# Second mixture of a decoder kernel: GpSimd issues the experts' row gathers further ahead of the scatters

## The chip, the cores and the metric

The kernel runs on one core of one Trainium2 chip. The metric is device time in microseconds (us) of one execution. A core has five instruction streams that matter here: TensorE (PE) for matmuls, VectorE (DVE), ScalarE (ACT), GpSimd (POOL) and SyncE (SP). POOL and SP start DMA transfers; the core's 16 DMA engines carry them out. POOL is the only one that issues indirect transfers, which take their row numbers from a tile of indices: a gather reads 128 rows of 1 KB out of DRAM into a tile, a scatter writes the 128 rows of a tile to rows of DRAM.

## What is computed

Two decoder layers, post-norm, over `x` of shape 8 x 256 x 256. Each has an attention, a cross-attention and a mixture of experts, each followed by a residual sum and a layer norm. The change lies in the mixture of the second layer only:

```python
probs = jax.nn.softmax(x @ gate_w.T, axis=-1)          # x: 2048 tokens x 256
top2_w, top2_idx = jax.lax.top_k(probs, 2)             # each token picks 2 of 8 experts
cap = int(1.25 * N / E)                                # 320 rows for each expert
buf = zeros((E, cap + 1, H)).at[a_e, p].set(x_a)       # the rows of each expert
h = silu(einsum('ech,efh->ecf', buf, w1) + b1)
y = einsum('ecf,egf->ecg', h, w2) + b2
contrib = y[a_e, p] * (a_w * valid)[:, None]           # back to the tokens, weighted
out = contrib.reshape(N, 2, H).sum(axis=1)
```

## The kernel before

All engines run programs written out by hand, with semaphores between them. Everything up to the last cross-attention takes the first 1,050 us or so and is the same in both kernels. Then comes the second mixture.

**The tiles.** The 8 experts have 320 rows each, so 2560 rows, which lie in 20 tiles of 128 rows. Two experts share five tiles: an even expert needs tiles 0 to 2 of its five, an odd one tiles 2 to 4. `tiles_of(e, True)` says which tiles are gathered for expert `e`: three for an even expert, two for an odd one (the third is there already). `tiles_of(e, False)` says which tiles are complete and can be scattered once expert `e` is computed: two for an even one, three for an odd one.

**TensorE**, for each expert `e`: wait for the weights (`t_w`), compute the hidden units (L1973, 8 matmuls of 320 columns, raising `e_u` after the fourth and the eighth), turn the rows of expert `e+1` (`turn1`, L1957, which waits for the gathers by `t_in{e % 4}` and raises `e_X`), wait for ScalarE's activation (`e_h`), compute the output (L1983, 12 matmuls, raising `e_y`). **VectorE** copies the turned rows (L1315), spreads some weights (L1332), and adds the bias to the output (L1321), which writes the tiles `y1t` and raises `e_ys`. **ScalarE** applies the activation (L782); it waits for `e_u`, and for `e_y` of the expert two before.

**GpSimd** issues the transfers of rows (L1468 to L1485). It waits once for the indices and for the rows that SyncE sent to DRAM (`sent1`). Then it issues the gathers of experts 0 to `XBUFS - 1`, that is of four experts (10 transfers). Then, for each expert, it waits for `e_ys` and scatters the complete tiles, and after it gathers for expert `e + 4`. Its queue is strictly in order. All 20 gathered tiles have places of their own in `x1t`, as have the 20 of `y1t`; nothing is written twice, so that only the four counting semaphores `t_in0` to `t_in3` are shared by two experts each.

**SyncE** loads the weights of experts 0 to 3 ahead of all this, those of expert `e + 4` when `e_ys` says that expert `e` is done (L584 to L587, four transfers, two of 256 KB, one of 128 KB and a small one), waits until all 20 scatters have landed (`e_out`), fetches the rows back in the order of the tokens (L596), and stores the result (L600).

After the last expert TensorE adds the residual (L1990), runs some matmuls that only keep it busy (L2008), and mixes the fetched rows (L1998).

Of the kernel before, what the change touches and what calls it, by code (L numbers as in the profile page):

```python
# [32 lines left out]
E, FH = 8, 512  # L33
# [16 lines left out]
XBUFS = 4  # L50
# [3 lines left out]
HOTS = 2 * EARLY  # L54
LATE_CHOOSE, LATE_RANK, LATE_HOTS, LATE_TABLE, LATE_QUANTA, LATE_RAW, LATE_INDEX, LATE_WEIGHTS = 0, 2, 3, 5, 6, 8, 8, 9
FAR = 128 * P
HIDDEN = 3
IDLE, IDLE_SPLIT, IDLE_CLIP = 96, 4, (4, 6)
IDLE_TURN, IDLE_LAYERS, IDLE_ROWS, IDLE_SCORES, IDLE_RESULT, IDLE_MIXED, IDLE_ROUTE = 4, 50, 20, 4, 12, 24, 2
# [171 lines left out]
def build_program(nc, dram, out, early0, sent0, sent1, outs0, outs1):  # L231
    with ExitStack() as ctx:
# [5 lines left out]
        def S(name):  # L238
            if name not in sems:
                sems[name] = ctx.enter_context(nc.semaphore(name))  # L240
            return sems[name]
# [212 lines left out]
        def tiles_of(e, gathered):  # L454

            first = PAIR1 * (e // 2)
            cut = PAIR1 // 2 + (1 if gathered else 0)
            return range(first + cut, first + PAIR1) if e % 2 else range(first, first + cut)

        def rows_at(e):  # L460

            k = e % XBUFS
            unread = 1 + (k < 2)
            return 16 * (len(range(k, TILES0, XBUFS)) + unread + sum(len(tiles_of(x, True)) for x in range(k, e + 1, XBUFS)))
# [902 lines left out]
        def _(pool):  # L1367
# [24 lines left out]
            def hide(p, n, c, u):  # L1392

                if c.selfattn and u < HIDDEN:
                    pool.wait_ge(S(f"h_PT{p}"), c.exps_at(n) + u + 1)
# [72 lines left out]
                play(order, stages | {"store": lambda p, n: store1(p, n)})  # L1468

            def gather1(e):  # L1470
                for j in tiles_of(e, True):
                    g.indirect_dma_start(x1t[:, j, :], None, sent1[:, :], bass.IndirectOffsetOnAxis(ap=idx1[:, j:j + 1], axis=0)
                                         ).then_inc(S(f"t_in{e % XBUFS}"), 16)

            pool.wait_ge(S("indexed"), 3)
            pool.wait_ge(S("sent1"), 16 * 2 * B)
            for e in range(XBUFS):
                gather1(e)
            for e in range(E):
                for i, j in enumerate(tiles_of(e, False)):  # L1480
                    pool.wait_ge(S("e_ys"), e + 1 + (i if e + 1 == E else 0))
                    g.indirect_dma_start(outs1[:, :], bass.IndirectOffsetOnAxis(ap=idx1[:, j:j + 1], axis=0), y1t[:, j, :], None
                                         ).then_inc(S("e_out"), 16)
                if e + XBUFS < E:
                    gather1(e + XBUFS)  # L1485
            for b in range(B):
                ln = lnrow[:, b]
                pool.wait_ge(S("vars"), b + 1)
# [619 lines left out]
```

## Time and profile before

| | us |
|---|---|
| median of 3 executions | 1147.88 (1147.74 to 1155.54) |
| the profiled execution | 1150.01 |
| its span, first to last instruction | 1148.3 |
| second mixture: first gather to last store | 1054.7 to 1148.3 |
| its eight experts on TensorE, first matmul to last | 1060.2 to 1117.9 |

The span is what the trace shows; the time of an execution lies 1.7 us above it. In the trace, times are counted from the start of the span. A busy share is the share of a stretch in which the engine worked. "Idle before" an instruction is how long its engine stood, and the arrow names what ended the wait. A releaser called "remote", or "another core or an unknown queue" in the chain, is one that the profile could not tie to a recorded instruction's end; the kernel uses one core.

### The profile page before, as it was taken

To read this page: it belongs to the slowest core of one execution; us is meant where nothing else is said; L and a number is where in the kernel's file an instruction comes from. 1 tells how busy PE (TensorE), PEld (TensorE's weight loads), DVE (VectorE), ACT (ScalarE), POOL (GpSimd) and SP (SyncE) were. 2 spreads that over 40 slices of the span, in tenths; PEclk is the share of its full clock that TensorE was granted. 3 is DMA by queue.
4 is the path that set the end of the run, shared out by engine and by line. 5 is a ranking of instruction groups with operands and counts; after the bars stand their busy time and mean duration, and the time that the engine had idled before them with its cause. 6 is when DMAs were issued, how large, how long until landed. Compare 5 with 4: busy or idle time off the path is not lost.

```text
span 1148.3 us, 20834 instructions
## 1 busy us (share of the span) xinstructions
PE 1013.1 (88%) x8628; PEld 723.1 (63%) x8628; DVE 617.3 (54%) x1398; ACT 425.2 (37%) x557; POOL 255.9 (22%) x282
## 2 busy tenths in 40 slices
PE   6889889889998898999998798989888987986887
PEld 3666566566565798997445465756556574753656
DVE  2653753753867463333334845665574759755333
ACT  1533533533513445555541244152406323340212
POOL 0310310310210223333332130231103111202642
PEclk9999999999988898999999899999999999997999
DMA  6014313213201971111112000200010010005427
GB/s 186 1 42 149 109 42 125 69 42 121 73 1 32 370 237 37 47 47 47 47 43 92 1 5 2 83 2 6 16 59 2 6 37 1 2 1 152 151 88 233
DMA packets 64238, 80.50 MB, mean 70 GB/s; under 512 B 12736, under 2 KB 57681, under 8 KB 63121
## 3 DMA queue, kind: packets, MB, share of 16 engines
q1 hardware_dynamic: 53392, 61.15, 16.1%
q0 software_dynamic: 5664, 15.47, 4.2%
q10 hardware_dynamic: 5088, 2.56, 0.9%
q8 instruction: 68, 1.11, 0.4%
q14 instruction: 26, 0.21, 0.1%
HBM read 46.13 MB, written 33.03 MB: 69 GB/s over the span
## 4 chain that ended last, share of the span: by engine, by line
PE 44%; issue 21%; DVE 16%; ACT 12%; SPq 2%; DMA 2%; POOL 2%; another core or an unknown queue 1%; ACTq 0%; DVEq 0%; POOLq 0%
PE ps L1511 8%; DVE sb_arena L865 6%; ACT sb_arena L642 6%; PE ps L1647 5%; PE ps L1669 3%; PE ps L1717 3%; PE ps L1772 3%; DVE sb_arena L869 3%; PE ps L1619 2%; PE ps L1983 2%; DVE ps L886 2%; PE ps L1555 1%; SPq L433 1%; PE ps L1998 1%
## 5 line engine op out<-in xcount | busy, mean ns | idle before, releaser
L642 ACT ACTIVATE sb_arena<-ps 77x2048 f32<-77x2048 f32 (+1 forms) x64 | 116.7, 1880 | 28.2 <-PE ps L1601 27.0
L1377 POOL TENSOR_TENSOR sb_arena<-sb_arena,sb_neghalf 128x2 f32<-128x2 f32 x40 | 28.7, 719 | 398.1 <-DVE sb_arena L831 398.1
L1511 PE MATMUL ps<-sb_arena,sb_wreg 128*128 128x256 f32 (+1 forms) x512 | 109.0, 361 | 6.8 <-issue 3.8
L1846 PE MATMUL ps<-sb_arena 128*128 128x128 f32 x800 | 104.4, 287 | 2.4 <-ACT sb_arena L750 2.1
L1846 PEld LDWEIGHTS ps<-sb_arena 128*128 128x128 f32 x800 | 101.2, 203 | 4.5 <-ACT sb_arena L750 2.8
L1511 PEld LDWEIGHTS ps<-sb_arena,sb_wreg 128*128 128x128 f32 (+1 forms) x512 | 88.0, 193 | 23.3 <-issue 8.3
L1619 PE MATMUL ps<-sb_arena 32*77 32x256 f32 (+1 forms) x1024 | 79.4, 428 | 25.3 <-ACT sb_arena L642 12.7
L750 ACT ACTIVATE sb_arena<-sb_arena 128x1024 f32 x72 | 76.0, 1056 | 17.1 <-issue 13.1
L1619 PEld LDWEIGHTS ps<-sb_arena 32*77 32x77 f32 (+1 forms) x1024 | 45.0, 179 | 45.8 <-ACT sb_arena L642 23.7
L865 DVE TENSOR_REDUCE sb_arena<-ps 128x8 f32<-128x2048 f32 x32 | 71.1, 2285 | 3.5 <-PE ps L1575 3.5
L1452 POOL DMA_INDIRECT outs<-sb_arena,sb_idx x36 | 36.3, 1010 | 145.6 <-ACT sb_arena L740 145.6
L1555 PE MATMUL ps<-sb_headrow,sb_identb 128*32 128x512 bf16 (+1 forms) x266 | 63.7, 376 | 1.4 <-DVE sb_arena L869 1.3
L892 DVE RECIPROCAL sb_arena<-ps 128x32 f32<-128x32 f32 x24 | 8.6, 358 | 100.7 <-PE ps L1655 99.2
L632 ACT ACTIVATE sb_nmTb<-ps 128x256 bf16<-128x256 f32 x24 | 9.2, 382 | 143.6 <-PE ps L1593 143.6
L1647 PE MATMUL ps<-sb_arena,sb_va 77*32 77x256 f32 (+1 forms) x1024 | 58.5, 381 | 3.0 <-ACT sb_arena L642 2.5
L1717 PE MATMUL ps<-sb_wreg,sb_arena 128*128 128x512 f32 x128 | 59.3, 623 | 0.2 <-DVE sb_arena L917 0.2
L1398 POOL TENSOR_SCALAR_AFFINE_SELECT sb_arena<-sb_arena 128x512 f32<-128x512 f32 x48 | 29.6, 648 | 124.5 <-ACT sb_arena L642 124.5
L869 DVE TENSOR_REDUCE sb_arena<-ps 128x16 f32<-128x1232 f32 x32 | 45.4, 1438 | 21.2 <-PE ps L1580 21.0
L837 DVE TENSOR_SCALAR sb_arena<-sb_arena 128x256 f32<-128x256 f32 x80 | 39.2, 531 | 27.4 <-POOL sb_arena L1377 27.2
L1669 PE MATMUL ps<-sb_wreg,sb_arena 128*128 128x256 f32 x192 | 45.2, 384 | 5.6 <-ACT sb_arena L650 5.6
L1647 PEld LDWEIGHTS ps<-sb_arena,sb_va 77*32 77x32 f32 (+1 forms) x1024 | 31.4, 110 | 27.3 <-ACT sb_arena L642 8.7
L1572 PE MATMUL ps<-sb_arena 32*128 32x256 f32 x512 | 36.7, 400 | 13.2 <-DVE sb_arena L865 13.2
(285 smaller groups left out, 1890.4 us busy)
## 6 DMA issues: line engine op xcount, KB each, us to landing
sb_arena<-in_m_w SPq DMA_DIRECT2D x8, 1536.0 KB, 10.7
sent<-sb_xres SPq DMA_DIRECT2D x32, 256.0 KB
sb_arena<-outs SPq DMA_DIRECT2D x16, 512.0 KB, 6.3
outs<-sb_zeros SPq DMA_DIRECT2D x4, 1664.0 KB, 9.8
sent<-sb_zeros SPq DMA_DIRECT2D x2, 2560.0 KB, 13.7
sb_arena<-in_m_w SPq DMA_DIRECT2D x16, 256.0 KB
early<-sb_xres SPq DMA_DIRECT2D x12, 256.0 KB, 2.9
sb_arena<-in_xT SPq DMA_DIRECT2D x8, 256.0 KB, 3.4
```

The costliest lines, as they stand in the source:

```text
L642: nc.scalar.activation(dst, src, ACT.Exp).then_inc(S(f"h_PT{p}"), 1)
L750: nc.scalar.activation(arena[:, WORDS * WORK + 1024 * part:WORDS * WORK + 1024 * (part + 1)], arena[:, bass.ds(blk * WORDS + 1024 * part, ...
L837: ins = v.tensor_scalar(dst[:, t, :], src[:, t, :], b.mv[:, t, 0:1], b.rstd[:, t:t + 1], ALU.subtract, ALU.mult)
L865: v.tensor_reduce(b.nm[:, :, u].rearrange("p (t r) -> p r t", t=NT), bank(p, 0, RT).rearrange("p r (t k) -> p r t k", t=NT), axis=AX.X, op ...
L869: v.tensor_reduce(b.nm[:, u * RT:(u + 1) * RT, :], bank(p, 0, RT)[:, :, 0:G * M].rearrange("p r (g k) -> p r g k", g=G), axis=AX.X, op=ALU ...
L1511: ins = mm(dst[:, m * cols:(m + 1) * cols], wt[0:rows, k, m * P:(m + 1) * P], src[0:rows, k, 0:cols], start=(k == 0), stop=(k == KC - 1))
L1555: ins = mm(bank(p, n)[IDLE:P, first:], identb[:, IDLE:P], headrow[:, :, :].rearrange("p g k -> p (g k)")[:, first:], start=True, stop=True ...
L1619: ins = mm(bank(p, r)[0:c.keys, a * L:(a + 1) * L], key, b.q[rows_of(r), u // 2 if c.selfattn else u, :], start=(a == 0), stop=False, skip ...
L1647: ins = mm(bank(p, 2 + g // 2)[rows_of(r), (g % 2) * L:(g % 2 + 1) * L], b.va[0:c.keys, kt, g * RT + r, :], b.PT[0:c.keys, g, first:first ...
L1669: ins = mm(bank(p, 3)[:, t * D:(t + 1) * D], bufs[p].onT[:, k, t * P:(t + 1) * P], W[f"{c.name}_wo"][:, k, :], start=(k == 0), stop=(k == ...
L1717: ins = mm(bank(p, 2 + t), b.xT[:, k, t * P:(t + 1) * P], W[wt][:, k, :], start=(k == 0), stop=(k == KC - 1))
L1846: ins = mm(to[:, m * P:(m + 1) * P], w[:, k, m * P:(m + 1) * P], slots0[j % 2].xT[:, k, :], start=(k == 0), stop=(k == KC - 1))
```

## The change

GpSimd's part of the second mixture is written in another order. `AHEAD1 = 6` takes the place of `XBUFS = 4` for the gathers ahead of the loop, and in the loop the gather for expert `e + 6` stands ahead of the scatter of expert `e` and no longer behind it. Since the gather for expert 6 therefore also comes before the first scatter, 18 of the 20 gather transfers are now issued ahead of the first scatter, and the last two between the first and the second expert's scatters. From expert 4 on, a gather first waits until the gather of the expert four before has landed, so that the two do not count on one semaphore at once.

```diff
+AHEAD1 = 6
@@
             def gather1(e):
+                if e >= XBUFS:
+                    pool.wait_ge(S(f"t_in{e % XBUFS}"), rows_at(e - XBUFS))
                 for j in tiles_of(e, True):
                     g.indirect_dma_start(x1t[:, j, :], None, sent1[:, :], bass.IndirectOffsetOnAxis(ap=idx1[:, j:j + 1], axis=0)
                                          ).then_inc(S(f"t_in{e % XBUFS}"), 16)
 
             pool.wait_ge(S("indexed"), 3)
             pool.wait_ge(S("sent1"), 16 * 2 * B)
-            for e in range(XBUFS):
+            for e in range(AHEAD1):
                 gather1(e)
             for e in range(E):
+                if e + AHEAD1 < E:
+                    gather1(e + AHEAD1)
                 for i, j in enumerate(tiles_of(e, False)):
                     pool.wait_ge(S("e_ys"), e + 1 + (i if e + 1 == E else 0))
                     g.indirect_dma_start(outs1[:, :], bass.IndirectOffsetOnAxis(ap=idx1[:, j:j + 1], axis=0), y1t[:, j, :], None
                                          ).then_inc(S("e_out"), 16)
-                if e + XBUFS < E:
-                    gather1(e + XBUFS)
```

On GpSimd, from the second gather of the program's last part on, the queue of the kernel before reads as follows. L1472 are gathers, L1482 scatters; `x9` counts the transfers behind the first, and a bracket is a wait.

```order
L1472 DMA sb_arena<-sent,sb_idx 128x256 x9
L1482 DMA outs<-sb_arena,sb_idx 6656x256 [waits e_ys] x2
L1472 DMA sb_arena<-sent,sb_idx 128x256 x3
L1482 DMA outs<-sb_arena,sb_idx 6656x256 [waits e_ys] x3
L1472 DMA sb_arena<-sent,sb_idx 128x256 x2
L1482 DMA outs<-sb_arena,sb_idx 6656x256 [waits e_ys] x2
L1472 DMA sb_arena<-sent,sb_idx 128x256 x3
L1482 DMA outs<-sb_arena,sb_idx 6656x256 [waits e_ys] x3
L1472 DMA sb_arena<-sent,sb_idx 128x256 x2
L1482 DMA outs<-sb_arena,sb_idx 6656x256 [waits e_ys] x10
```

Gathers and scatters take turns, four times. The same stretch of GpSimd's queue in the changed kernel, where the gathers stand in L1475 and the scatters in L1487:

```order
L1475 DMA sb_arena<-sent,sb_idx 128x256 x9
L1475 DMA sb_arena<-sent,sb_idx 128x256 [waits t_in0]
L1475 DMA sb_arena<-sent,sb_idx 128x256 x2
L1475 DMA sb_arena<-sent,sb_idx 128x256 [waits t_in1]
L1475 DMA sb_arena<-sent,sb_idx 128x256
L1475 DMA sb_arena<-sent,sb_idx 128x256 [waits t_in2]
L1475 DMA sb_arena<-sent,sb_idx 128x256 x2
L1487 DMA outs<-sb_arena,sb_idx 6656x256 [waits e_ys] x2
L1475 DMA sb_arena<-sent,sb_idx 128x256 [waits t_in3]
L1475 DMA sb_arena<-sent,sb_idx 128x256
L1487 DMA outs<-sb_arena,sb_idx 6656x256 [waits e_ys] x18
```

Eight gathers have moved ahead of the first two scatters, two stand behind them, and the other 18 scatters follow with no gather between. The counts of transfers, 20 and 20, are the same; no other engine's program is touched.

## Rows read from the trace of the kernel before

**Rows 1.** The page: span, shares of the chain, first mixture's scatters.

```profile
span 1148.3 us, 20834 instructions
...
PE 44%; issue 21%; DVE 16%; ACT 12%; SPq 2%; DMA 2%; POOL 2%; another core or an unknown queue 1%; ACTq 0%; DVEq 0%; POOLq 0%
...
L1452 POOL DMA_INDIRECT outs<-sb_arena,sb_idx x36 | 36.3, 1010 | 145.6 <-ACT sb_arena L740 145.6
```

**Rows 2.** The chain in order of time: start, us, what, from 1030 us on.

```profile
1057.40 2.60 DMA sb_arena<-sent,sb_idx
...
1077.70 7.09 another core or an unknown queue
...
1091.57 7.38 another core or an unknown queue
...
1121.18 2.42 DMA outs<-sb_arena,sb_idx
```

**Rows 3.** TensorE's timeline: start, us, what, idle before it and its releaser.

```profile
1077.76 3.00 PE L1983 MATMUL ps<-sb_arena 128*128 128x256 f32 x12 [0.18 <-ACT sb_arena L782]
...
1085.85 3.01 PE L1983 MATMUL ps<-sb_arena 128*64 128x256 f32 x12 [2.08 <-ACT sb_arena L782]
...
1091.62 3.00 PE L1983 MATMUL ps<-sb_arena 128*128 128x256 f32 x12 [0.18 <-ACT sb_arena L782]
...
1101.69 4.44 PE L1983 MATMUL ps<-sb_arena 128*64 128x256 f32 x12 [4.06 <-ACT sb_arena L782]
...
1108.91 3.00 PE L1983 MATMUL ps<-sb_arena 128*128 128x256 f32 x12 [0.18 <-ACT sb_arena L782]
```

**Rows 4.** VectorE's timeline, the bias of experts 2 and 4.

```profile
1084.03 1.08 DVE L1321 TENSOR_TENSOR sb_arena<-ps,sb_arena 128x256 f32<-128x256 f32 x3 [4.90 <-remote]
...
1096.82 1.08 DVE L1321 TENSOR_TENSOR sb_arena<-ps,sb_arena 128x256 f32<-128x256 f32 x3 [3.86 <-remote]
```

**Rows 5.** Waits from 1050 us on: in total, times, longest.

```profile
ACT sb_arena L782 <- remote: 16.2, 3, 7.5
...
DVE sb_arena L1321 <- remote: 8.8, 2, 4.9
...
PE ps L1957 <- DMA sb_arena<-sent,sb_idx: 0.4, 1, 0.4
```

**Rows 6.** Stretches: us, busy time by engine, TensorE's clock, DMA share, GB/s.

```profile
1060.00:1065.00 5.00, 3.55 (x18) 2.58 (x18) 0.96 (x1) 1.28 (x1) 3.78 (x5) 1.00 0.35 105
1071.98:1074.99 3.01, 3.01 (x14) 2.25 (x14) 1.98 (x5) 0.00 (x0) 2.40 (x3) 1.00 0.77 254
1077.76:1080.76 3.00, 3.00 (x13) 1.97 (x13) 1.37 (x5) 0.00 (x0) 2.09 (x4) 1.00 0.89 307
1085.85:1088.86 3.01, 3.01 (x13) 2.25 (x14) 1.00 (x5) 0.00 (x0) 2.40 (x3) 1.00 0.75 243
1091.62:1094.62 3.00, 3.00 (x13) 1.97 (x13) 1.34 (x5) 0.00 (x0) 2.17 (x3) 1.00 0.91 299
1101.69:1106.13 4.44, 4.44 (x13) 2.95 (x14) 1.74 (x5) 0.00 (x0) 0.00 (x0) 0.66 0.00 0
```

**Rows 7.** GpSimd's timeline: tenth gather, first scatter, and later ones.

```profile
1066.20 0.95 POOL L1472 DMA_INDIRECT sb_arena<-sent,sb_idx  x1 [0.30 <-issue]
1070.41 1.00 POOL L1482 DMA_INDIRECT outs<-sb_arena,sb_idx  x1 [3.26 <-DVE sb_arena L1321]
...
1097.00 0.96 POOL L1472 DMA_INDIRECT sb_arena<-sent,sb_idx  x1 [0.30 <-issue]
...
1118.63 0.97 POOL L1482 DMA_INDIRECT outs<-sb_arena,sb_idx  x1 [2.02 <-DVE sb_arena L1321]
```

**Rows 8.** SyncE's timeline: weight loads of experts 5, 6 and 7.

```profile
1076.25 0.89 SPq L584 DMA_DIRECT2D sb_arena<-in_m_w  x2
...
1085.13 0.89 SPq L584 DMA_DIRECT2D sb_arena<-in_m_w  x2
...
1090.11 0.89 SPq L584 DMA_DIRECT2D sb_arena<-in_m_w  x2
```

## The prediction

> **What bounds the kernel now.** The page says that the chain of work over the whole kernel runs mostly on TensorE (44%), with GpSimd at 2% [rows 1]. So I looked only at the second mixture, which is all that the change touches, and there first at TensorE's timeline. Its second matmul group (L1983) starts at 1077.76, 1085.85, 1091.62, 1101.69 and 1108.91 us for experts 2 to 6 [rows 3]. The cycles between them are 8.09, 5.77, 10.07 and 7.22 us. An expert costs 5.77 us when nothing is late, and then TensorE bounds the loop with an idle of 0.18 us [rows 3]. Two cycles are long because TensorE stood still ahead of L1983, 2.08 us for expert 3 and 4.06 us for expert 5, each time for ScalarE's activation. One is long because L1983 itself took 4.44 us and not 3.00 [rows 3]; the granted clock over that group was 0.66 [rows 6], that is, part of it ran at 1.2 and not at 2.4 GHz, right behind the idle of 4.06 us. The sum of what is lost here is 2.08 + 4.06 + 1.44 = 7.58 us.
>
> ScalarE was not slow. The table of waits says that it and VectorE waited for something "remote", 16.2 us in three waits and 8.8 us in two [rows 5], and the chain has 7.09 us from 1077.70 and 7.38 us from 1091.57 that it can tie to nothing [rows 2]. VectorE's case is the cleanest: the bias of expert 2 waits for `e_y` and nothing else, the matmul group that raises it ended at 1077.76 + 3.00 = 1080.76, and VectorE began at 1084.03, 3.27 us later [rows 3, 4]. For expert 4 it is 1094.62 against 1096.82, 2.20 us late. So what is late is the news from TensorE, or TensorE's own work is later than the record says. Neither a gather nor a weight load is being waited for: TensorE waited for a gather once, for 0.4 us [rows 5].
>
> When is it late? The four groups of L1983 for experts 1 to 4 lay beside DMA shares of 0.77, 0.89, 0.75 and 0.91 [rows 6], and the two late ones are those at 0.89 and 0.91. GpSimd's gathers alone make 0.35 [rows 6]. In both late stretches a weight load (issued at 1076.25 and at 1090.11 [rows 8]) ran beside GpSimd's transfers, three scatters of an odd expert with gathers ahead of and behind them. In the first mixture 36 scatters came with 145.6 us of idle ahead of them [rows 1], some 4 us ahead of each, and no "remote" wait is listed there. I take the crowd of transfers for the cause. That is a reading, not something the trace shows.
>
> **The change part by part.** Nothing is added or removed on any engine but waits on GpSimd.
>
> *Gathers of experts 4, 5 and 6 ahead of the first scatter (8 transfers).* The tenth gather starts at 1066.20 and takes 0.95, with 0.30 to the next [rows 7]: eight more need 8 x 1.25 = 10.0 us and end at 1077.45. Before, GpSimd stood idle for 3.26 us of that time, ahead of the first scatter [rows 7]; now it does not.
>
> *The new waits on `t_in`.* A gather lands 2.60 us behind its start [rows 2]. Expert 4's gather waits for expert 0's, expert 5's for expert 1's, and so on, always with at least seven transfers, 8.7 us, between. The price is nothing. The cover is these 8.7 us against 2.6; behind the waiting instruction stand all further gathers and scatters, and SyncE's fetch behind the last scatter. The bounds are 0 and, if each were paid in full, 4 x 2.6 = 10.4 us of GpSimd's time, of which the slack below takes all.
>
> *The first scatters are later.* That of expert 0 goes from 1070.41 to 1077.45. Two scatters, two gathers, three scatters and two scatters at 1.29 us bring GpSimd through expert 2 at 1077.45 + 9 x 1.29 = 1089.1. Expert 3's tiles are ready when SyncE's load starts, 1090.11 [rows 8]. From there GpSimd waits for VectorE again, as before. Nobody waits for a single scatter: the fetch waits for all 20, and the last three start at 1118.63 because VectorE makes them ready then [rows 7]. The slack is 1118.6 - 1089.1 = 29 us, so the tail, from the last matmul group to the end, keeps its length. Cost 0; if the cover were gone each scatter would cost 1.29 us.
>
> *Gathers earlier than they are needed.* With one wait of 0.4 us for a gather in the trace, that of the first [rows 5], there is nothing to gain from data that come sooner. Value 0, at most 0.4 us.
>
> *What lies beside the weight loads.* This is the only term that can move the time. The load of expert 5 (from 1076.25) still meets GpSimd's unbroken row of transfers: gather 6, scatter 0, gather 7. I leave that stretch as it is, 2.08 us. The load of expert 7 (from 1090.11) met gather 6, three scatters and gather 7, and GpSimd ran without a pause until its last gather at 1097.00 [rows 7]. Now the gathers are gone from there and the scatters of expert 3 only begin at 1090.11; with 2.4 us from issue to landing [rows 2] their data moves from about 1092 on. So a third or more of the 3 us of L1983 has no GpSimd traffic. An estimate from the rows: 0.91 - 0.35/3 = 0.79, next to the 0.77 and 0.75 that went unpunished. So I take away the 4.06 us and with it the slow 1.44 us, for the clock fell behind that idle.
>
> The Trainium skill speaks against this term. Its page "DMA: Bandwidth & Descriptors" (Issuing engines are not separate DMA queues) says that transfers from GpSimd, ScalarE and SyncE all end up on the same 16 DMA engines and interleave there, and "SBUF — State Buffer" says that the DMA side and the engines' side of the memory cannot contend and that TensorE and ScalarE never wait for anyone there. By these pages a crowd of transfers could not hold up TensorE at all, and the sum would be 0. The "remote" waits show that something did [rows 5], and the pages name no other cause.
>
> **The sum.** -4.06 - 1.44 = -5.5 us. Against the profiled execution (span 1148.3 [rows 1], time 1150.0) this gives a span of 1142.8. The median of the runs, 1147.9, is 2.1 us below the profiled execution, so the forecast is 1147.9 - 5.5 = 1142.4 us.
>
> **The rivals.** A, the forecast: the second late stretch goes, the first stays. 1142.4 us.
>
> B: the lateness does not come from the gathers, or it just moves, and the total is the same; this is also what the two pages of the skill would give. For it: the bytes and their number do not change, and the load of expert 5 is as crowded as before. Against it: the shares of 0.75 and 0.77 without and of 0.89 and 0.91 with lateness. 1147.9 us.
>
> C: both late stretches go, because what hurts is gathers and scatters in turn on one queue, and there are only three changes between the kinds left instead of nine. 1147.9 - 7.6 = 1140.3 us. Against it: the first late stretch keeps two gathers between scatters.
>
> D, the other side: what hurts is the length of GpSimd's unbroken row of transfers. In the trace of before, it was 10 transfers from 1070.41 until the first lateness and there it cost 2.08 us; a second row of 12 cost 5.5. Now it is 10 + 8 + 9 = 27 in one row, from 1054.7 to 1089. If lateness comes with every ten or so beside a load, the loads of experts 4, 5 and 6 all meet it: two more stretches at 2.08 us, while the last goes or stays, so between -5.5 + 4.2 and +4.2, and up to +5.5 if one of them is like the bad one. It decides from the point where the loads at 1070 and 1085 are hit too. I take 1152 us. Against it: ten gathers in a row at the start, without a load beside them, disturbed nobody.
>
> **How the numbers follow.** A 0.40, B 0.32, D 0.18, C 0.10. The range must hold A, B and C, with the partial cases of D: from 1140.3 less 1 us of scatter to about 1150.5, which leaves out most of D's upper end and little else. For this kernel a measurement tells about 1%, 11.5 us, from no change. None of the cases reaches that: the most there is to win in this loop is 7.6 us, and D's worst, with every load hit at 5.5 us, would need two more bad stretches than before. So faster by over 1% gets 0.02, slower by over 1% 0.02, and within 1% 0.96.
>
> **What would show it.** In the changed kernel's trace, GpSimd's first scatter at about 1077.5 with no idle ahead of it, and its first idle near 1089; no wait of TensorE for a gather beyond 0.4 us; L1983 of expert 3 still behind some 2 us of idle; L1983 of expert 5 with 0.2 us ahead of it, 3.0 us long and the clock at 1.00. If "remote" waits stand at another expert, the term is wrong in place; if they sum to the same, B holds; if TensorE's idle ahead of L1983 comes at experts 2 and 4, D does. The forecast is wrong at its root if the lateness has nothing to do with the transfers.

## The result and the profile after

| | before | changed |
|---|---|---|
| median | 1147.81 us (1141.91 to 1155.54, 12 runs) | 1157.35 us (1152.56 to 1162.10, 12 runs) |
| ratio to before | | 1.0097, 95% interval 1.0079 to 1.0116 |
| profiled execution | 1150.01, span 1148.3 | 1154.70, span 1153.0 |
| first gather to first L1489 (changed: L1492) | 1054.72 to 1131.18: 76.5 us | 1051.17 to 1135.87: 84.7 us |

The changed kernel is 9.5 us slower, inside 1%, and 15 us above the forecast of 1142.4. The last line of the table is the stretch that the change can reach, up to GpSimd's first instruction in the last layer norm (L1489); it is 8.2 us longer. Behind it both kernels take 17.1 us to the end.

In the changed kernel `L1986` is the old L1983, L1976 the hidden matmuls (old L1973), L1960 the transposes (L1957), L783 ScalarE's activation (L782), L1316 and L1322 VectorE's copy and bias (L1315, L1321), L1475 a gather, L1487 a scatter. TensorE's timeline of the changed kernel, with columns as in [rows 3]:

```profile
1062.43 3.00 PE L1986 MATMUL ps<-sb_arena 128*128 128x256 f32 x12 [0.86 <-ACT sb_arena L783]
1065.36 2.42 PE L1976 MATMUL ps<-sb_arena 128*128 128x320 f32 x8
1067.62 0.82 PE L1960 MATMUL ps<-sb_ident,sb_arena 128*128 128x128 f32 x6
1081.26 5.68 PE L1986 MATMUL ps<-sb_arena 128*64 128x256 f32 x12 [12.82 <-ACT sb_arena L783]
...
1090.10 3.00 PE L1986 MATMUL ps<-sb_arena 128*128 128x256 f32 x12 [0.18 <-ACT sb_arena L783]
...
1096.07 3.01 PE L1986 MATMUL ps<-sb_arena 128*64 128x256 f32 x12
```

There is one hole where before had two, and it is larger: 12.82 us of idle ahead of expert 1's second group, and then 5.68 us for a group that takes 3.01 [rows 3]. The loss is 12.82 + 2.67 = 15.5 us against 7.58 before, 7.9 more. From expert 2 on every cycle is undisturbed: the two late stretches of before, at experts 3 and 5, are gone, both of them.

The waits (from 1050 us on: total, times, longest), the chain in order of time, and VectorE's bias of expert 0 and copy for expert 1:

```profile
ACT sb_arena L783 <- remote: 17.8, 2, 12.8
...
DVE sb_arena L1316 <- remote: 13.0, 1, 13.0
...
DVE sb_arena L1322 <- remote: 5.0, 1, 5.0
...
PE ps L1960 <- DMA sb_arena<-sent,sb_idx: 0.4, 1, 0.4
```

```profile
1062.38 12.67 another core or an unknown queue
...
1075.66 5.00 another core or an unknown queue
```

```profile
1068.09 1.08 DVE L1322 TENSOR_TENSOR sb_arena<-ps,sb_arena 128x256 f32<-128x256 f32 x3 [4.98 <-remote]
1082.12 0.96 DVE L1316 COPY sb_arena<-ps 128x768 f32<-128x768 f32 x1 [12.96 <-remote]
```

ScalarE's two activations for expert 1:

```profile
1075.13 0.53 ACT L783 ACTIVATE sb_arena<-ps,sb_arena 128x320 f32<-128x320 f32 x1 [12.75 <-remote]
1080.68 0.53 ACT L783 ACTIVATE sb_arena<-ps,sb_arena 128x320 f32<-128x320 f32 x1 [5.02 <-remote]
```

It is the same kind of lateness as in [rows 2, 4, 5]: VectorE's bias needs the group that ended at 1062.43 + 3.00 = 1065.43 and begins 2.66 us later. ScalarE's two activations need the first four and all eight matmuls of L1976, and the record has all eight ended by 1067.78; they begin at 1075.13 and at 1080.68, the second 12.9 us late. No gather is waited for beyond the old 0.4 us. GpSimd's timeline, columns as in [rows 7]:

```profile
1072.67 0.95 POOL L1475 DMA_INDIRECT sb_arena<-sent,sb_idx  x1 [0.30 <-issue]
1073.92 1.00 POOL L1487 DMA_INDIRECT outs<-sb_arena,sb_idx  x1 [0.30 <-issue]
1075.23 0.99 POOL L1487 DMA_INDIRECT outs<-sb_arena,sb_idx  x1 [0.30 <-issue]
1076.52 0.99 POOL L1475 DMA_INDIRECT sb_arena<-sent,sb_idx  x1 [0.30 <-issue]
1077.82 0.96 POOL L1475 DMA_INDIRECT sb_arena<-sent,sb_idx  x1 [0.31 <-issue]
1088.45 1.00 POOL L1487 DMA_INDIRECT outs<-sb_arena,sb_idx  x1 [9.67 <-DVE sb_arena L1322]
```

SyncE's timeline has the loop's first weight load:

```profile
1069.19 0.89 SPq L585 DMA_DIRECT2D sb_arena<-in_m_w  x2
```

From 1051.17 to 1078.78 GpSimd issued 22 transfers, one every 1.25 to 1.30 us and without a pause. TensorE's news came late from 1065.4 on; the last of it reached ScalarE at 1080.68 and VectorE at 1082.12, 1.9 and 3.3 us behind the end of that row. Finally the stretches (columns as in [rows 6]):

```profile
1062.43:1065.43 3.00, 3.00 (x13) 1.97 (x13) 0.68 (x4) 0.00 (x0) 2.16 (x3) 1.00 0.31 87
1068.44:1081.26 12.82, 0.00 (x0) 0.00 (x1) 0.72 (x3) 1.05 (x2) 7.90 (x9) 0.58 0.47 147
1081.26:1086.94 5.68, 5.68 (x13) 3.81 (x14) 1.74 (x5) 0.00 (x0) 0.00 (x0) 0.50 0.01 3
1101.85:1104.85 3.00, 3.00 (x13) 1.97 (x13) 1.33 (x5) 0.00 (x0) 1.95 (x2) 1.00 0.94 306
```

The group whose signal came late lay beside a DMA share of 0.31, and one beside 0.94, more than any in [rows 6], was on time. So the crowd of transfers beside a group, by which I had told late from punctual, does not tell them apart. And the granted clock was 0.58 on average over the 12.82 us in which TensorE did nothing and 0.50 (1.2 GHz) over the group behind them, which took 5.68 us instead of 3.01.

### The profile page after: what moved, and what is told of

Its sections match the earlier page's. It is cut to its first block, busy times and chain, and to the rows that moved or that the text cites. A ratio compares the mean times of both kernels' runs of the same rounds, so it can differ in the third digit from the quotient of the medians.

```text
span 1153.0 us, 20834 instructions
## 1 busy us (share of the span) xinstructions
PE 1009.6 (88%) x8628; PEld 720.5 (62%) x8628; DVE 617.9 (54%) x1398; ACT 425.6 (37%) x557; POOL 255.8 (22%) x282
## 4 chain that ended last, share of the span: by engine, by line
PE 44%; issue 21%; DVE 16%; ACT 12%; DMA 2%; POOL 2%; another core or an unknown queue 2%; SPq 1%; ACTq 0%; DVEq 0%; POOLq 0%
PE ps L1514 8%; DVE sb_arena L866 6%; ACT sb_arena L643 6%; PE ps L1650 5%; PE ps L1672 3%; PE ps L1720 3%; PE ps L1775 3%; DVE sb_arena L870 3%; PE ps L1986 2%; PE ps L1622 2%; DVE ps L887 2%; PE ps L1558 1%; PE ps L1976 1%; PE ps L2001 1%
## 5 line engine op out<-in xcount | busy, mean ns | idle before, releaser
L1849 PE MATMUL ps<-sb_arena 128*128 128x128 f32 x800 | 101.3, 282 | 2.2 <-ACT sb_arena L751 1.9
L1849 PEld LDWEIGHTS ps<-sb_arena 128*128 128x128 f32 x800 | 98.1, 198 | 4.3 <-ACT sb_arena L751 2.7
```

Of the source, the lines that this page charges most:

```text
L1849: ins = mm(to[:, m * P:(m + 1) * P], w[:, k, m * P:(m + 1) * P], slots0[j % 2].xT[:, k, :], start=(k == 0), stop=(k == KC - 1))
```

## The experiments

All kernels are compared with runs of the kernel before on the same chip. The stretch "first gather to first L1489" (or its line in each kernel), called the loop below, is worked out from the starts of these two instructions in each trace.

### First four: what in the new order does it

**e1_four_only**, the changed kernel without the gathers of experts 4 to 7, whose rows stay unwritten:

```diff
-            for e in range(AHEAD1):
+            for e in range(XBUFS):
                 gather1(e)
...
-                if e + AHEAD1 < E:
-                    gather1(e + AHEAD1)
...
-                pe.wait_ge(S(f"t_in{e % XBUFS}"), rows_at(e))
+                pe.wait_ge(S(f"t_in{e % XBUFS}"), rows_at(e % XBUFS))
```

> The changed kernel without the ten gathers of experts 4 to 7: GpSimd gathers for experts 0 to 3 only, and TensorE turns what lies in the other ten tiles of x1t from earlier work (so the rows of experts 4 to 7 are not the right ones). All scatters and weight loads stay. Theory G (TensorE is held up while gathers beyond the first ten are under way, the scatters and loads are harmless): no 'remote' wait is left, every cycle of L1986 is 5.8 to 6.0 us, and the time is that of the kernel before less its 7.6 us of loss, about 1140 us. Theory K of the prediction (the crowd of all transfers, above a DMA share of 0.85): the loads of experts 5 and 7 still meet scatters, so at least one of the lateness stretches stays, with 2 to 5 us, and the time is 1143 to 1148 us.

Measured: 1145.23 us, ratio 0.9984 (0.9952 to 1.0016), no remote wait in the table of waits, loop 68.6 us, 7.9 shorter than before's. Its TensorE:

```profile
1062.31 3.00 PE L1984 MATMUL ps<-sb_arena 128*128 128x256 f32 x12 [0.86 <-ACT sb_arena L783]
...
1068.28 3.01 PE L1984 MATMUL ps<-sb_arena 128*64 128x256 f32 x12
...
1074.06 3.00 PE L1984 MATMUL ps<-sb_arena 128*128 128x256 f32 x12 [0.18 <-ACT sb_arena L783]
```

With 10 gathers in one row and then two or three scatters at a time nothing is late, though the weight loads are all there. The trace is that of theory G, but the median is only 3.2 us below before's, its interval includes no change, and by the time alone it lies in the range of theory K (1143 to 1148). The profiled execution gives 4.8 of the 7.9 us back at its end (21.9 us behind the loop instead of 17.1); what that was, no run here shows.

**e2_ahead8** (`AHEAD1 = 8`, all 20 gathers first) and **e3_ahead4** (`AHEAD1 = 4`, so that only the order within the loop differs from before):

```diff
-AHEAD1 = 6
+AHEAD1 = 8
```

> The changed kernel with AHEAD1 = 8: all 20 gathers stand ahead of the first scatter. Theory G: the held-up stretch begins at the same place as in the changed kernel (from about the eleventh gather on, some 11 us after the first) and ends some 3 us after the twentieth gather's issue; since no two scatters lie in between any more, it ends 2.6 us earlier, and the time is 1152 to 1157 us. Theory R (gathers and scatters in turn are what hurts): with no scatter between gathers nothing is held up, about 1140 us. Theory K: no change against the changed kernel, 1157 us.

> The changed kernel with AHEAD1 = 4: ten gathers ahead as in the kernel before, and then the gather of expert e + 4 ahead of the scatter of expert e and not behind it. Theory G: what costs is how many late gathers TensorE's work meets in one stretch; here three follow at once on the first ten, and the rest come in three groups of two and three, each ahead of a scatter. The lateness is spread as in the kernel before, with a total of 6 to 10 us, so 1146 to 1151 us. If only the distance of gathers from the first ten mattered (theory T, a busy row longer than ten), the first group alone would be late, and the time about 1143 us.

Measured: e2 1158.07 us, ratio 1.0063 (1.0032 to 1.0093), loop 84.9; e3 1150.53 us, ratio 1.0002 (0.9977 to 1.0026), loop 76.5. The late group of e2, and then the two of e3:

```profile
1088.49 5.60 PE L1986 MATMUL ps<-sb_arena 128*64 128x256 f32 x12 [13.74 <-ACT sb_arena L783]
```

```profile
1075.38 4.65 PE L1986 MATMUL ps<-sb_arena 128*64 128x256 f32 x12 [2.35 <-ACT sb_arena L783]
...
1097.03 4.40 PE L1986 MATMUL ps<-sb_arena 128*128 128x256 f32 x12 [2.66 <-ACT sb_arena L783]
```

The place and the size go with GpSimd's rows. In e2 the row is again 22 transfers from the first gather on (20 gathers and two scatters), and the hole is that of the changed kernel. In e3 the first row is 13 transfers long, and a smaller hole stands already at expert 1, where before had none behind its row of 10. Theory G had e3 right (1146 to 1151 us) and e2 too low (1152 to 1157); theories R and T, which had e2 at 1140 and e3 at 1143, fail.

**e4_mirror**, the changed kernel with the gathered tiles in the opposite order of places:

```diff
-                    g.indirect_dma_start(x1t[:, j, :], None, sent1[:, :], bass.IndirectOffsetOnAxis(ap=idx1[:, j:j + 1], axis=0)
+                    g.indirect_dma_start(x1t[:, TILES1 - 1 - j, :], None, sent1[:, :], bass.IndirectOffsetOnAxis(ap=idx1[:, j:j + 1], axis=0)
```

(the transposes read from the same places).

> The changed kernel with the 20 gathered tiles in mirrored places: tile j at place 19 - j of x1t, so that the first ten gathers write where the last ten wrote before. Order, count and size of all transfers are the same. Theory P (it is where a gather writes: the places of tiles 10 to 19 are those that disturb TensorE): the held-up stretch moves to the first ten gathers, which lie beside little work of TensorE (from about 1056 us on), and the late ten are harmless: TensorE's signals of expert 0 are late by some us, those of expert 1 are not, and the time is 1142 to 1150 us. Theories G, K and T: no change against the changed kernel, 1155 to 1159 us.

Measured: 1156.04 us, ratio 1.0065 (1.0043 to 1.0086), 14.45 us of idle ahead of expert 1's group:

```profile
1082.16 5.48 PE L1986 MATMUL ps<-sb_arena 128*64 128x256 f32 x12 [14.45 <-ACT sb_arena L783]
```

Where in the memory the gathers write is not the cause.

So far one reading fitted all: the news from TensorE is late once GpSimd has issued some ten transfers without a pause, until a few us behind the row. (The first late signal of each row fell at the ninth and the eighth transfer in before, the groups' ends at 1080.76 and 1094.62, and at the twelfth in the changed kernel, 1065.43.) That a gather past the tenth is under way is not enough: in before, VectorE copied the rows for expert 4 on time, 0.04 us behind L1957 (1090.84 + 0.60 = 1091.44), with the gathers of 1088.02, 1089.31 and 1090.58 just issued, in a row that was then five transfers long:

```profile
1091.48 0.69 DVE L1315 COPY sb_arena<-ps 128x512 f32<-128x512 f32 x1 [1.39 <-PE ps L1957]
```

But all the long rows on these chips hold such gathers, and e1 left out the gathers as well as the row, so it cannot tell a row of any kind from a row with gathers in it. The next four were to break the row.

### Second four: breaking the row

**e5_ahead6_pauses**, one line behind the gathers of each expert in the changed kernel; **e6_before_pauses**, the same in before for experts 4 to 7 only:

```diff
                 for j in tiles_of(e, True):
                     g.indirect_dma_start(...
                                          ).then_inc(S(f"t_in{e % XBUFS}"), 16)
+                pool.wait_ge(S(f"t_in{e % XBUFS}"), rows_at(e))
```

> The changed kernel with one wait more: behind the two or three gathers of each expert GpSimd waits until they have landed, so that its gathers come in rows of two or three (the two scatters that stand between gathers may lengthen one row to five or six) and not in one row of 22 transfers. Everything else stays: six experts' gathers stand ahead of the first scatter. Row theory (TensorE's signals become late once GpSimd has issued some ten or more transfers without a pause, and stay so until the row has landed): no wait of ScalarE or VectorE for something remote, L1986 of expert 1 follows within 0.5 us, the stretch from the first gather to the first L1492 falls from 84.7 us to about 69, and the time from 1157.4 to 1141 to 1146. Rival one (it is the number of gathers that stand ahead of the first scatter, or simply what TensorE does at that point of the loop, whatever GpSimd's pauses): 12 us or more of idle ahead of L1986 of expert 1 as in the changed kernel, 1154 to 1159. Rival two (the total of transfers per time in the window of some 15 us counts, not the break): about half the lateness, 1148 to 1153.

> The kernel before with a wait for the landing behind the gathers of experts 4 to 7 only, so that its two rows of 10 and 12 transfers become rows of at most five or six; the first row of ten gathers stays. Row theory: both late stretches (2.08 us and 4.06 us of idle, 1.44 us of slow clock) go, and the stretch from the first gather to the first L1492 falls from 76.5 us to about 69; time 1140.5 to 1145, a ratio of 0.993 to 0.998. Rival (the lateness has to do with the weight loads or with the gathers of late experts themselves, not with the unbroken row): remote waits stay at 5 us or more, 1147 to 1149.

**e7_ahead6_work**, the changed kernel with GpSimd at work in the gaps instead (and SyncE's last fetch behind it):

```diff
+                g.memset(yg_all[:, 2 * e:2 * e + 2], 0.0).then_inc(S("memsets"), 1)
```

> The changed kernel with GpSimd kept at work between the groups of gathers: behind each expert's gathers it writes 128 x 1024 zeros to a region that nobody reads before it is written again (work added, nothing left out; I guess 1 us each from the 0.65 us of its 128 x 512 select). It never rests, but its transfers come in groups of two or three. If what hurts is that GpSimd is busy without a rest, TensorE's signals are late at least as long as in the changed kernel, from about 14 us behind the first gather until behind the last gather (36 us): 15 to 25 us lost, 1157 to 1168. If only transfers issued back to back hurt, there are no remote waits and 1141 to 1146. If transfers per time count, part of it stays: 1148 to 1154.

**e8_scatter_row**, e5 with `AHEAD1 = 8` and one wait ahead of the loop:

```diff
+            pool.wait_ge(S("e_ys"), 5)
             for e in range(E):
```

> All 20 gathers first, each expert's followed by a wait for its landing (rows of two or three), and no scatter before expert 4's results are ready; then GpSimd has 12 scatters to issue in one row, at 1.29 us each 15.5 us, from about 40 us behind the first gather. Row theory, whatever the kind of transfer: nothing late until about 50 us behind the first gather, then remote waits of some 4 to 8 us in sum until the row has landed at about 57 us; 1145 to 1152. If only gathers can make it (they write the memory beside TensorE) or only a mix of the two: no remote wait at all, 1141 to 1146. The last scatters are not later than the results of expert 7, so that the tail should keep its length.

| | median | ratio (95%) | loop |
|---|---|---|---|
| before, beside them | 1141.84 | | |
| e5 | 1153.72 | 1.0100 (1.0073 to 1.0127) | 79.7 |
| e6 | 1146.30 | 1.0039 (1.0025 to 1.0053) | 73.6 |
| e7 | 1142.11 | 0.9999 (0.9984 to 1.0013) | 68.7 |
| e8 | 1152.01 | 1.0090 (1.0058 to 1.0121) | 79.3 |

None of the four has a remote wait, and e7's TensorE and GpSimd look like this:

```profile
1063.45 3.00 PE L1988 MATMUL ps<-sb_arena 128*128 128x256 f32 x12 [0.86 <-ACT sb_arena L784]
...
1069.42 3.01 PE L1988 MATMUL ps<-sb_arena 128*64 128x256 f32 x12
```

```profile
1055.89 0.96 POOL L1478 MEMSET sb_arena<- 128x1024 f32 x1
1057.02 0.95 POOL L1476 DMA_INDIRECT sb_arena<-sent,sb_idx  x1 [0.16 <-issue]
```

I would have called the row theory shown by this. The number that did not fit was that of the kernel before: 1141.84 us on this chip, against 1147.81 beside the result and 1148.41 beside e1 to e4. A kernel with a perfect loop (e7) was no faster than it.

The three that were slower had lost by their own pauses, e8 like e5 (first scatter 43.3 us behind the first gather, the last scatters issued too late for the tail to keep its place, against what I had expected); and its long row of scatters, on this chip, says nothing on whether scatters alone can do it. In e5 GpSimd waits for each landing, and the first scatter starts 39.5 us behind the first gather, where the changed kernel has it after 22.8; GpSimd's queue then ends last. Two of its rows:

```profile
1061.85 0.94 POOL L1475 DMA_INDIRECT sb_arena<-sent,sb_idx  x1 [2.03 <-DMA sb_arena<-sent,sb_idx]
...
1095.66 1.00 POOL L1488 DMA_INDIRECT outs<-sb_arena,sb_idx  x1 [3.52 <-DMA sb_arena<-sent,sb_idx]
```

In e6 it is TensorE that waits for rows which come too late:

```profile
1095.65 0.87 PE L1959 MATMUL ps<-sb_ident,sb_arena 128*128 128x128 f32 x6 [1.22 <-DMA sb_arena<-sent,sb_idx]
...
1103.88 0.66 PE L1959 MATMUL ps<-sb_ident,sb_arena 128*128 128x128 f32 x4 [2.27 <-DMA sb_arena<-sent,sb_idx]
```

That my expectations gave e5 and e6 the time of a perfect loop was a second miss: neither expectation priced the pauses or followed what four or eight of them do to the queue.

### The next four: is it the chip?

**b1_before_again** and **b2_after_again** are the two kernels, word for word. **e9_before_work** is before with e7's memset. **e10_one_break** is the changed kernel with one memset behind the tenth gather:

```diff
+                if e == XBUFS - 1:
+                    g.memset(yg_all[:, 2 * e:2 * e + 2], 0.0).then_inc(S("memsets"), 1)
```

> The kernel before, word for word, profiled once more beside the others on this chip. In the last batch the kernel before had a median of 1141.8 us, and 1148.4 in the batch before that, while a kernel without any late signal (e7_ahead6_work) had 1142.1. Theory one, the lateness depends on the chip: where the median of before is near 1142 its profile shows no remote wait and a stretch from first gather to first L1489 of about 69 us; where it is near 1148 the profile shows the two late stretches of 5 to 8 us in sum. Theory two, it is always there and the 6 us lie elsewhere (then e7_ahead6_work loses them elsewhere too): the two late stretches stand in the profile whatever the median. The ratio to the runs of before is 1.000 by construction.

> The changed kernel, word for word, profiled once more on this chip. If the lateness comes with the unbroken row of 22 transfers on every chip: some 13 to 16 us lost at expert 1, ratio 1.007 to 1.013. If it depends on the chip, and this one is of the quick sort: no remote wait, ratio 0.998 to 1.002.

> The kernel before with only the write of 128 x 1024 zeros behind each expert's gathers (work added, nothing left out), which took about 0.8 us each in e7_ahead6_work. No row of back-to-back transfers is then longer than five or six; no wait is added. Row theory: no remote wait, loop of about 69 us from the first gather to the last matmul group's follower, 1140 to 1142 where before takes 1148 (ratio 0.993 to 0.995), and no difference on a chip where before is not late. Rival (the number of transfers in some 10 to 15 us counts and not the break, since these breaks lower the rate only from one in 1.28 us to one in 1.6 us): half the lateness stays, ratio 0.996 to 0.999.

> The changed kernel with one single write of 128 x 1024 zeros (0.8 us) behind the tenth gather, so that the row of 22 becomes one of 10 and one of 12. If a short break starts the count anew: TensorE's signals are on time until some 10 to 13 us behind the break (about 24 us behind the first gather) and late from there to the end of the row, as in the second row of before: 3 to 6 us lost, 1146 to 1150, ratio about 1.000. If a break of 0.8 us is too short to count (what matters is an average over many transfers): late from 14 us as in the changed kernel, 12 us or more, 1154 to 1158, ratio 1.006 to 1.010.

| | median | ratio (95%) | loop |
|---|---|---|---|
| before, beside them | 1142.19 | | |
| b1 | 1141.10 | 1.0005 (0.9985 to 1.0026) | 68.4 |
| b2 | 1141.79 | 1.0005 (0.9980 to 1.0030) | 68.7 |
| e9 | 1141.54 | 1.0003 (0.9978 to 1.0027) | 68.6 |
| e10 | 1142.28 | 1.0007 (0.9979 to 1.0036) | 69.0 |

Before again, the groups of experts 3 and 5 that were late in [rows 3]:

```profile
1083.99 3.01 PE L1983 MATMUL ps<-sb_arena 128*64 128x256 f32 x12
...
1095.74 3.01 PE L1983 MATMUL ps<-sb_arena 128*64 128x256 f32 x12
```

The changed kernel again, and GpSimd's first rest in it:

```profile
1067.90 3.00 PE L1986 MATMUL ps<-sb_arena 128*128 128x256 f32 x12 [0.86 <-ACT sb_arena L783]
...
1073.87 3.01 PE L1986 MATMUL ps<-sb_arena 128*64 128x256 f32 x12
...
1095.80 0.96 POOL L1487 DMA_INDIRECT outs<-sb_arena,sb_idx  x1 [1.31 <-DVE sb_arena L1322]
```

Here 30 transfers in one row, from 1056.66 until the rest of 1.31 us that ended at 1095.80, hold up nobody: no remote wait, not one group late. On this chip the same program loses nothing, before or changed. The breaks of e7, e9 and e10 can show nothing where there is nothing to break.

### The last six: looking for a chip where it is late

**e11_work_again** is e7 and **e12_one_break_again** e10, word for word. **e13_half_rows** is the changed kernel with gathers of half the bytes (the other half of each row is left out):

```diff
-                    g.indirect_dma_start(x1t[:, j, :], None, sent1[:, :], bass.IndirectOffsetOnAxis(ap=idx1[:, j:j + 1], axis=0)
+                    g.indirect_dma_start(x1t[:, j, 0:P], None, sent1[:, :].rearrange("r (a b) -> (r a) b", b=P), bass.IndirectOffsetOnAxis(ap=idx1[:, j:j + 1], axis=0)
```

> The kernel e7_ahead6_work word for word (a write of 128 x 1024 zeros behind each expert's gathers, so that no row of back-to-back transfers is longer than five), to see it on another chip. On a chip of the late sort (runs of before near 1148 us): row theory, no remote wait and 1140 to 1142, a ratio of 0.993 to 0.996 where the changed kernel had 1.0097; rival (a break of 0.8 us does not count, or the number of gathers ahead of the first scatter does it), 8 us or more lost, ratio 1.004 or more. On a chip of the quick sort (runs of before near 1142 us): ratio 0.998 to 1.002 by every theory, and the run says only how common that sort is.

> The kernel e10_one_break word for word (one write of 128 x 1024 zeros behind the tenth gather; rows of 10 and 12). On a chip of the late sort: if a short break starts the count anew, on time until about 24 us behind the first gather and then late to the end of the row, 3 to 6 us lost, ratio 0.999 to 1.003; if it does not, late from 14 us on, 12 us or more lost, ratio 1.006 to 1.010. On a chip of the quick sort: 0.998 to 1.002, no remote wait.

> The changed kernel whose gathers fetch 128 of the 256 columns of a row (the other half of each row is left out and stays stale, and the half that is fetched is that of another row), so that a gather moves 64 KB and not 128 KB; the number of gathers, their row of 18 and the scatters are as in the changed kernel. On a chip of the late sort: if the count of transfers, or GpSimd's time in issuing them without a break, does it, late as in the changed kernel, 12 us or more, ratio 1.006 to 1.010; if the bytes in flight do it, late by less than half, ratio 0.994 to 1.001. On a chip of the quick sort: 0.998 to 1.002, no remote wait.

Measured, beside before at 1142.37: 1142.45, ratio 1.0015 (0.9994 to 1.0036); 1141.16, 0.9992 (0.9970 to 1.0015); 1139.55, 0.9985 (0.9963 to 1.0007). No remote wait in any. Half the bytes change nothing on a chip without lateness, which says nothing on what they do where there is some.

**e14_one_break_third** (e10) and **e15_work_third** (e7), once more:

> The kernel e10_one_break once more, for want of a chip of the late sort in the last two batches. On such a chip (runs of before near 1148 us), if a short break starts the count anew: TensorE's signals are on time until about 24 us behind the first gather and late from there to the end of the row, 3 to 6 us lost, ratio 0.999 to 1.003; if it does not: late from 14 us on, 12 us or more lost, ratio 1.006 to 1.010. On a chip of the quick sort (runs of before near 1142 us): 0.998 to 1.002 and no remote wait.

> The kernel e7_ahead6_work (a write of 128 x 1024 zeros behind each expert's gathers) once more, in search of a chip of the late sort. There (runs of before near 1148 us): no remote wait and a ratio of 0.993 to 0.996 if short breaks end the lateness; 8 us or more lost and a ratio of 1.004 or more if they do not. On a chip of the quick sort (runs of before near 1142 us): 0.998 to 1.002 and no remote wait.

Measured: 1143.65 beside 1139.22, ratio 1.0022 (0.9997 to 1.0046); 1143.08 beside 1142.38, ratio 0.9997 (0.9973 to 1.0021). No remote wait in either, loops of 68.8 and 68.5 us.

**e16_after_third**, the changed kernel once more:

> The changed kernel word for word, on whatever chip comes. If the lateness belongs to some chips alone: runs of before near 1142 us go with a ratio of 0.998 to 1.002 and no remote wait, runs of before near 1148 us go with a ratio of 1.007 to 1.013 and some 13 us of idle ahead of L1986 of expert 1. Against that theory stands a chip with runs of before near 1142 us and a ratio of 1.006 or more, or one with a remote wait in the profile.

Measured: 1158.44 us beside before at 1150.71, ratio 1.0065 (1.0041 to 1.0088), loop 85.4 us. Its late group and its wait:

```profile
1085.31 5.68 PE L1986 MATMUL ps<-sb_arena 128*64 128x256 f32 x12 [13.80 <-ACT sb_arena L783]
```

```profile
ACT sb_arena L783 <- remote: 18.8, 2, 15.1
```

All chips together, with the chip's number where the record has it (it has none for the result's):

| | runs of before | changed kernel | in the profiles |
|---|---|---|---|
| the chip of the result | 1147.81 | 1157.35 | late, before and changed |
| e1 to e4 (chip 7) | 1148.41 | (e2 1158.07, e4 1156.04) | late in e2, e3 and e4, not in e1 |
| e5 to e8 (chip 0) | 1141.84 | | none late |
| b1 to e10 (chip 13) | 1142.19 | 1141.79 | none late, before or changed |
| e11 to e13 (chip 10) | 1142.37 | | none late |
| e14 (chip 9) | 1139.22 | | none late |
| e15 (chip 0 again) | 1142.38 | | none late |
| e16 (chip 3) | 1150.71 | 1158.44 | late |

The medians of before lie 5.4 to 11.5 us lower where nothing is late, and what its trace had lost was 7.58 us. The changed kernel is 1141.8 there against 1157.35 and 1158.44, 15.6 and 16.7 more, and its traces had lost 15.5 and 13.80 + 2.67 = 16.5. Both gaps have about the size of the holes; the chips differ by some us otherwise too (1139.22 to 1142.38 among the quiet ones). Chip 0 was quiet twice, but no numbered late chip was met twice, so that it is the chip, and not something else that differed between these sessions, is the simplest reading and not shown.

## Why the prediction was wrong

- *Where the kernel loses:* right for the chip of the profile. The forecast took 2.08 + 4.06 + 1.44 = 7.58 us out of [rows 3] as lost to late news from TensorE. A loop without any late signal is 68.4 to 68.7 us long against 76.5, 7.8 to 8.0 us shorter (e1, b1, b2).
- *The first scatter and GpSimd's row:* nearly right. Eight gathers at 1.25 us put the first scatter at 1077.45 in the time of before, 22.7 us behind the first gather; it came 22.75 us behind it, with no idle ahead. That GpSimd would work without a pause through expert 2's scatters, 34.4 us, was only seen where nothing was late (37.8 us in b2); on the late chip it stopped after 27.6 us and stood for 9.67.
- *The new waits cost nothing:* right, every gather in the row follows the last by 0.30 or 0.31 us. The landing was not priced well: the 2.6 us from [rows 2] are those of a gather of expert 0; later in the loop it took up to 0.95 + 3.52 = 4.5 us (e5). The cover of 8.7 us was enough for that too.
- *Slack 29 us, tail unchanged, earlier rows worth nothing:* right; 17.1 us from the first L1492 to the end of the span in both, and 0.4 us of waiting for a gather as before. No time came from the gathers being early: on the one quiet chip where both ran, the changed kernel was no faster (b1, b2).
- **The step that failed:** "I take the crowd of transfers for the cause", and with it the term of -4.06 - 1.44 = -5.5 us, and a sum that has no term for a new late stretch. The four shares of [rows 6] happened to order themselves by lateness, 0.75 and 0.77 against 0.89 and 0.91; the changed kernel has groups on time at 0.94 and a late one at 0.31. The two late stretches of before did go, 7.58 us of them, and a new one of 15.5 us came at expert 1. The sum should have been -7.6 + 15.5 = +7.9, beside a loop 8.2 us longer and a median 9.5 us longer. (The spans differ by 4.7 us alone, because in the profiled execution of the changed kernel the first gather came 3.5 us earlier.)
- **The rival that held in kind, as far as these runs go, was D**, the length of the unbroken row, on 0.18. Its place and size were wrong: its sign was idle at experts 2 and 4, and the hole came at expert 1; I priced every ten transfers at one stretch of 2.08 us, and only beside a weight load. The row of 22 made one hole of 12.8 us, and the news was late before the first load of the loop was issued at 1069.19, so a load need not lie beside it; then came the slow clock of the next group. That ten gathers in a row at the start disturbed nobody was true and was no argument against D: in before, TensorE raised no signal between 1065.15, at the ninth of these gathers, and 1069.01, 1.9 us behind the last, so there was nothing that could have been late. VectorE had both on time:

```profile
1065.19 0.69 DVE L1315 COPY sb_arena<-ps 128x512 f32<-128x512 f32 x1 [3.01 <-issue]
...
1069.05 1.08 DVE L1321 TENSOR_TENSOR sb_arena<-ps,sb_arena 128x256 f32<-128x256 f32 x3 [2.39 <-PE ps L1983]
```

- **What no rival had:** that the lateness is there on some chips only. B (nothing changes, 0.32) is what b1 and b2 show on a quiet chip, 1141.1 against 1141.8 us. The rules of the Trainium skill that the prediction weighed, in "DMA: Bandwidth & Descriptors" (Issuing engines are not separate DMA queues: what the engines issue is interleaved on one set of DMA engines) and in "SBUF — State Buffer" (SBUF: two separate sides: the DMA side does not contend with the engines), gave a sum of 0. The quiet chips agree, with 30 transfers in a row and no late signal; the late chips do not, though what is late there need not be the memory that these pages speak of.
- *The range* reached to 1150.5 because D's upper end was capped by two stretches of 2.08 us. The row that should have widened it was the 7.38 us in [rows 2]: beside a row of 12 transfers one piece of the chain was already that long, and 22 is far outside what the trace had shown.

What stays open: why TensorE's news is late behind such a row, and whether it is the signal that is late or TensorE's own work, with ends that the record has too early; why on some chips only; whether a row without late gathers does it; whether a break in the row removes it there (e7, e9 and e10 were meant for that and never met such a chip; e1 and e3 only show that shorter rows lose less); and whether the transfers' number, bytes or time counts. That the row is the cause is argued from five orders on late chips (before, changed, e1, e2, e3), in which the holes came and went with it, and not from an edit that changes the row's length alone. No version here beats both kernels: the orders with breaks are equal to before where nothing is late, and untried where it is.

## What to carry to other kernels

When a trace has waits that it ties to nothing, count what stood unbroken ahead of each of them as well as how busy the machine was beside it: two late and two undisturbed groups will fit almost any measure. A change that makes a sequence longer than any in the trace needs a rival with no ceiling from that trace. And run both kernels on more than one chip before a difference of 1% is called theirs: here the same two programs had a ratio of 1.0097 on one chip and of 1.0005 on another.

## What the runs showed of the hardware

- In three sessions (that of the result, that of e1 to e4, that of e16; two or three chips) signals from TensorE reached VectorE and ScalarE late, by the record of TensorE's ends, when GpSimd issued long rows of indirect DMAs back to back, one in 1.25 to 1.30 us. A first row of 10 was harmless in before and in e1, where no signal of TensorE fell between its ninth transfer and 1.9 us behind its end; other rows of 10 to 13 cost 2.1 to 5.5 us each (before, e3), and rows of 22 cost 15.5 to 16.9 us (changed, e2, e4, e16), the slower clock behind them included. On four other chips nothing was late, on one of them with a row of 30.
- GpSimd, waiting for its gathers to land, stood 2.0 to 2.1 us each time before the loop's first weight load, 3.0 to 3.5 us the four times behind it, and 2.10 us the last time (e5).
- TensorE's granted clock was 0.58 on average over 12.8 us without a matmul and 0.50 over the group behind them, which took 5.68 instead of 3.01 us (changed); behind an idle of 2.08 us it kept 3.01 [rows 3], and the hole of 2.35 us in e3 was followed by a group of 4.65.
